# Feed-forward stage: the place of VectorE's mixes for the next batch among its maskings and additions

## The reference

```python
x_mixed = k[0] * xp[:, :-2] + k[1] * xp[:, 1:-1] + k[2] * xp[:, 2:]   # a mix over three positions
h = jnp.einsum('bsd,pdm->bspm', x_mixed, W1) + b1                     # 9 paths of 64
stacked_paths = jnp.einsum('bspm,pmd->bspd', h, W2) + b2
scores = jnp.tanh(x_mixed @ Wo1 + bo1) @ Wo2 + bo2
weights = jax.nn.one_hot(jnp.argmax(scores, axis=-1), P)              # one path per position
collapsed = jnp.einsum('bspd,bsp->bsd', stacked_paths, weights)
return _layernorm(x + collapsed, gamma, beta)
```

## Time and profile before

| what | value |
|---|---|
| median of the runs | 1507.09 us (three runs, 1502.43 to 1507.27) |
| the profiled execution, its own time | 1502.06 us |
| its span, first to last instruction | 1500.3 us |
| TensorE, weight loads, VectorE, ScalarE, GpSimd busy | 95%, 44%, 73%, 64%, 29% |
| mean granted clock of TensorE | 0.992 of full |

### The profile page before, as it was taken

One profiled execution on the slowest core, in us unless ns is written; L12 is line 12 of the kernel. 1 busy time (PEld: TensorE's weight loads), 2 busy tenths in 40 slices (PEclk: granted clock), 3 DMA queues, 4 the chain that ended last, 5 costly groups with the idle time before them and its releaser, 6 DMA issues. The chain is left out here.

```text
span 1500.3 us, 25145 instructions
## 1 busy us (share of the span) xinstructions
PE 1423.4 (95%) x8234; PEld 656.3 (44%) x8282; DVE 1102.5 (73%) x2647; ACT 960.6 (64%) x2121; POOL 431.4 (29%) x561
## 2 busy tenths in 40 slices
PE   7999989999999999999999999999988999999995
PEld 4665543333333333333333333333324666566654
DVE  3225658888888888888888888888733888878775
ACT  4655447777777777777777777777775445455532
POOL 3443232122133133133133133123243262122312
PEclk9999999999999999999999999999999999999998
DMA  7899674223643843842842842842714521110001
GB/s 224 265 296 292 205 217 111 87 63 95 156 89 95 181 92 90 185 93 85 190 93 80 195 94 74 200 95 66 143 23 130 92 85 57 43 56 28 15 29 43
DMA packets 166752, 178.20 MB, mean 119 GB/s; under 512 B 26397, under 2 KB 135784, under 8 KB 166632
## 3 DMA queue, kind: packets, MB, share of 16 engines
q1 hardware_dynamic: 158184, 168.31, 44.2%
q10 hardware_dynamic: 8448, 8.39, 1.7%
HBM read 109.79 MB, written 66.06 MB: 117 GB/s over the span
## 5 line engine op out<-in xcount | busy, mean ns | idle before, releaser
L975 ACT ACTIVATE a_probs<-a_ps_s 128x512 f32<-128x512 f32 (+3 forms) x1536 | 648.0, 499 | 232.2 <-PE a_ps_s L1077 228.5
L176 DVE CUSTOM_DVE_ANT_0 h_space<-a_ps_m,a_causal 128x640 f32<-128x640 f32 (+5 forms) x624 | 530.3, 888 | 94.5 <-PE a_ps_m L150 91.1
L1077 PE MATMUL a_ps_s<-s_qs,s_ks 99*128 99x512 bf16 (+3 forms) x1536 | 405.6, 329 | 6.5 <-ACT a_probs L975 4.7
L150 PE MATMUL a_ps_m<-s_ks,s_qs 96*128 96x512 bf16 (+3 forms) x1440 | 347.1, 326 | 9.1 <-DVE a_mx L176 2.3
L925 POOL TENSOR_SCALAR_AFFINE_SELECT a_probs<-a_probs 128x512 f32<-128x512 f32 x256 | 163.0, 637 | 664.6 <-ACT a_probs L975 664.6
L1035 PE MATMUL a_ps_o<-a_probs,s_vq 128*32 128x512 f32 (+3 forms) x3072 | 327.6, 497 | 10.1 <-POOL a_probs L925 4.2
L1077 PEld LDWEIGHTS a_ps_s<-s_qs,s_ks 99*128 99x128 bf16 x1536 | 137.0, 97 | 330.7 <-ACT a_probs L975 241.6
L150 PEld LDWEIGHTS a_ps_m<-s_ks,s_qs 96*128 96x128 bf16 x1440 | 122.6, 98 | 157.8 <-issue 57.9
L1547 PE MATMUL f_ps_o<-f_w,f_hm 128*128 128x256 f32 (+1 forms) x640 | 151.5, 385 | 0.9 <-DVE f_y L1454 0.9
L1547 PEld LDWEIGHTS f_ps_o<-f_w,f_hm 128*128 128x128 f32 (+1 forms) x640 | 121.5, 192 | 27.6 <-issue 8.4
L545 PE MATMUL p_ps_qk<-p_x_t,p_wqk 128*128 128x512 f32 x256 | 120.5, 600 | 0.1
(11 more groups left out here) (137 smaller groups left out, 1310.6 us busy)
## 6 DMA issues: line engine op xcount, KB each, us to landing
qk_parts<-h_space SPq DMA_DIRECT2D x64, 384.0 KB, 4.0
s_qs<-qk_parts SPq DMA_DIRECT2D x192, 128.0 KB, 2.8
s_ks<-qk_parts SPq DMA_DIRECT2D x192, 128.0 KB, 2.8
v_rows<-h_space SPq DMA_DIRECT2D x16, 896.0 KB, 6.1
s_vq<-v_rows SPq DMA_DIRECT2D x32, 448.0 KB, 4.5
f_x_in<-in_L_attn_x_dram ACTq DMA_DIRECT2D x16, 512.0 KB, 6.7
heads_out<-a_o_sb SPq DMA_DIRECT2D x128, 64.0 KB
f_x_in<-in_L_attn_x_dram SPq DMA_DIRECT2D x8, 1024.0 KB, 8.8
```

The source lines that it names most:

```text
L150: last = pe.matmul(out, self.qs[0:TROWS, j, h, q], self.ks[0:TROWS, j, h, s:s + wide], start=k == 0, stop=mask is None)
L176: taken = dve.tensor_tensor_reduce(out=shown[:, i % 2, k * CHUNK:k * CHUNK + width], in0=row, in1=self.causal[:, SEQ - width:SEQ], scale=1 ...
L975: act.activation(probs[:, st % PB, h, 0:width], ps_s[:, n % BANKS, 0:width], ACT.Exp, scale=SCALE).then_inc(exps[h % 2], 1)
L1077: pe.matmul(ps_s[:, n % BANKS, 0:width], ks[0:MROWS, j, h, kt * P:(kt + 1) * P], qs[0:MROWS, j, h, q0:q0 + width], start=True, stop=True)\
```

## The change

VectorE's two mixes of the next batch no longer stand ahead of the first addition of x. The first addition comes first, then maskings 0, 1 and 2, the first mix, maskings 3 and 4, the second mix, and the second addition of x. Nothing else of the program is different.

```diff
                         if c == 0 and not last:
                             layernorm(1 - e, 8 * (b + e) + 16, at)
-                        if c == 1 and not last:
-                            for k in range(KC):
-                                mix(b + 1, 1 - e, k, at)
                         if c or not first:
                             add_x1(n - 1, *((e, 0) if c else (1 - e, 1)), 0)
                         for i in range(MC):
                             keep_hidden(n, c, i)
+                            if c == 1 and not last and i in (2, LAST):
+                                mix(b + 1, 1 - e, i // LAST, at)
                         if c or not first:
                             add_x1(n - 1, *((e, 0) if c else (1 - e, 1)), 1)
```

## The result

The changed kernel takes 1531.3 us (median of six runs, 1528.54 to 1536.17) against 1506.94 us for the kernel before: a ratio of 1.0172 (95% interval 1.0151 to 1.0192), so it is slower by 1.7%. The profiled execution took 1530.69 us for a span of 1529.0 us, 28.7 more than the profiled execution before, with a mean granted clock of 0.983 instead of 0.992. (The two medians lie 24.4 us apart; the part on the prediction says why.)

What follows compares the result with a forecast made beforehand. TensorE, busy 95% of the span, was taken to bound the kernel. The profiled 1502.1 us plus 15.0 for later starts and 10.1 for clock falls gave 1527.2 us, range 1513 to 1535.

Steps and rivals of the forecast that it cites:

- turn 1: Batch 1's turn, where GpSimd sums the last batch's attention: later start +0.8 us, plus 1.4 for slowed mixing instructions.
- the clock: TensorE's granted clock falls behind the new stall in all seven turns, six more than before, 1.69 us each: +10.1 us.
- my first reading: If the other runs before had two or three more clock falls, the new kernel gains nothing on top; otherwise 1532 us.
- The bound: TensorE is busy 95% of the span, so what counts is where it stands still or newly could.
- The comparison of 5.02 us of mixing with 1.63 us of room: VectorE's two waits in a first chunk, 0.54 and 1.09 us, are the room for 5.02 us of moved mixes.
- A: Start of VectorE's first addition of x when only TensorE holds it back, 2.47 us after output tile 1 starts.
- The chain from A: VectorE's addition, maskings and both mixes: next hidden product at A + 8.98 against TensorE's own A + 5.21, 3.8 us stall.
- The collision that goes: First mixing instruction, 3.14 us beside GpSimd's addition of beta, takes 1.28 us in the new place in turns 2 to 6.
- everything else, at nothing: ScalarE's products, bank release, second addition, normalization, roots, store and first chunks: no cost beyond shifting along.
- The clock holds: Rival: TensorE's clock does not fall and only the later start counts, 1517.1 us; few falls or none 0.23.
- GpSimd's collision comes along: Rival: a GpSimd operation meets the mixes in every turn from 1 on, 11.2 us more, 1538.4; 0.10 with longer low stretches.
- not slower: Rival: the mixes fit into VectorE's waits among the maskings, at most the 10.5 us of stalls go, 1491.6 us; 0.07.

Runs made afterwards that it cites:

- both mixes in the middle: The changed kernel with both mixes placed between maskings 2 and 3: 1515.14 us, ratio 1.0084 to the kernel before.
- The filled stall: The changed kernel with four more f32 products on TensorE at the end of each second chunk: 1523.2 us, ratio 1.0121 to the kernel before.
- one mix in the room: Against the kernel before, first mix left ahead of the first addition of x, second mix put between maskings 2 and 3: 1491.38 us, ratio 0.9909.
- second mix late: Against the kernel before, first mix left ahead of the first addition of x, second mix put behind the last masking: 1503.38 us, ratio 0.9993.
- short and long sums: The changed kernel with GpSimd's last-batch summing operations on one of sixteen heads each (short, 1527.98 us), or with each of its additions done twice (long, 1534.47 us).
- addition first: Against the kernel before, only the first addition of x moved ahead of both mixes, the maskings after them: 1539.08 us, ratio 1.022.

## Why the prediction held, and where it was off

The predicted 1527.2 lies 4.1 us under the measured 1531.3, in the range, on the right side. Part of the closeness is luck. Against the 28.7 us between the profiled executions I had 25.1: turn 1 came out 4.1 us too low and 1.5 us outside the changed part were missing, while the clock was 1.4 and the other six turns together 0.5 us too high.

*The 5 us between the profiled execution before and its median: the clock.* I had left open whether they come from further falls. Of the twenty executions of the kernel before that were timed beside the experiments, the five with a mean granted clock of 0.992 or 0.993 took 1499.9 to 1502.6 us, and the nine at 0.988 or 0.989 took 1505.0 to 1506.6. A clock lower by 0.004 over 1505 us is worth 6 us, by an estimate as rough as the three digits of the clock, and the groups differ by 4.5 us. The profiled execution before, at 0.992, belongs to the faster group, while the changed kernel's (1530.69) is near its median. That fits my first reading, that the new kernel gains nothing on top: the medians lie 24.4 us apart instead of 28.7, and of these 24.4 the clock's part is smaller than 8.7.

*The bound: right. The comparison of 5.02 us of mixing with 1.63 us of room: right in its answer, wrong as a measure.* The order with one mix behind A loses its stalls; the orders with two behind A all gain one. But one mix is 2.5 us, more than 1.63, and it fits. Maskings 3 and 4 and the second addition of x may slip behind the start of the opening product, whose first half waits for none of them, so VectorE's idle time is less than the room. What decides is the chain from A up to the last thing that the product waits for: with one mix behind masking 2 it is A + 5.27, against TensorE's own A + 5.21.

*The chain from A: right.* Forecast and measured start of the opening product: A + 8.98 and 8.86 in the changed kernel, 7.78 and 7.68 with both mixes in the middle. With the second mix behind the last masking it was 6.47 and 6.97, where masking 3's wait was left out; with one mix in the room the 5.20 measured is TensorE's own and says only that the chain is no longer. The stall came out at 3.4 to 3.5 us instead of 3.8. In turn 3 the product starts 0.12 us earlier than the chain said, and the stall begins with the modelled end of the output tile at A + 5.36, 0.15 us behind the A + 5.21 at which the product would start beside it. Later starts in turns 0 and 2 to 6: 12.3 us, forecast 3.7 + 9.1 = 12.8.

*Turn 1: mis-sized.* I gave its later start 0.8 + 1.4 = 2.2 us, at most 3.6, with each mixing instruction losing 0.35 us as in the earlier trace rows. It was 6.3, and the wait that I had put at up to 5 us was 9.1. The step that failed is to carry the loss per instruction from a place where the mixes were under way before GpSimd's run to one where they arrive within it. The Trainium skill (SBUF — State Buffer, SBUF: two separate sides) lets the one that started first keep the ports for its whole instruction; I took from it one operation per mixing instruction as the most. Here the hold lasted for nine operations, and for seventeen with the run made longer.

*The clock: right in kind, 1.4 us too high.* Six more falls at 1.69 us, 10.1 in all, against 8.7: five falls and not seven, but two of them cost 2.6 to 2.7 us. The rule that idle gaps between bursts of matmuls send the clock down (the Trainium skill, TensorE: Matmul & The Clock Gate, Why this matters for your kernels) would have had all seven turns fall; the trace has two stalls of 3.4 to 3.5 us without a fall. The filled stall settles that the stalls are the cause.

*The collision that goes and "everything else, at nothing": right.* The first mixing instruction is back at 1.27 us outside turn 1; no wait in the first chunks appeared, and the distance from the last opening product to the end grew by 0.2 us.

*Rivals.* "The clock holds" is out by the windows; "GpSimd's collision comes along" happened in one turn of six, through another of its operations than the one I had named; "not slower" is out for this order, and its price, 1491.6 (the old stalls gone and nothing in their place), is close to the 1491.4 of the order with one mix in the room. *Not foreseen*: 1.3 us ahead of the changed part, which no edit touches. Over the nine profiles the fourth spreading of the very first chunk starts anywhere from 1144.2 to 1148.3 us, so a difference of that size between two single profiles says nothing of the change.

## What to carry to other kernels

When work is moved behind a wait to shorten one stall, add up the engine's chain from that wait to the last thing that the next consumer needs, and compare it with the time at which the consumer would start by itself. Here that is 5.27 us with one mix against 5.21, and 7.78 or 8.98 with two, so one mix of two fits. Keep the part that is ready ahead of the wait, and count the engine's idle time at the wait as given away: here 4.7 us a turn. And price a long stall of TensorE (here 3.4 us and up) with the slower matmuls that follow it: 8.7 of the 28.7 us between the two profiles were that.

## What the runs showed of the hardware

*Stalls of TensorE and its granted clock.* From the profiles of the nine kernels, in the second chunks of this stage, falls from 1.00 (2.4 GHz) to 0.50 (1.2 GHz) by the longest stall in one piece:

| stall, us | kernels | falls |
|---|---|---|
| 0.3 or less | one mix in the room; stall filled, without turn 1 | 0 of 13 |
| 1.3 to 2.5, ahead of the fourth spreading | before | 1 of 6 |
| 1.5 to 2.0 | second mix late | 0 of 7 |
| 2.2 to 2.3 | both in the middle | 0 of 6 |
| 3.4 to 3.5 | changed, short and long sums | 15 of 19 |
| 4.2 | addition first | 6 of 6 |
| 5.6 to 14.4 | turn 1 of changed, addition first, both in the middle, long sums, stall filled | 5 of 5 |

Behind a stall of 3.4 to 3.5 us a fall makes the next 3.7 us of matmuls 1.7 or 2.6 us longer; behind the longer ones of turn 1, 1.4 to 2.7. What separates the four of nineteen, and the one at 1.56 us, these runs don't tell.

*VectorE held by GpSimd.* A mixing instruction has two inputs in SBUF. In five kernels one arrived in turn 1 within an undisturbed run of GpSimd operations and stood until the run was over: 6.87 us in the changed kernel and with both mixes in the middle, 6.86 with the stall filled, 8.61 with the addition first, 12.23 with the longer run. In the other three with a full run there (the kernel before and the two orders with the first mix ahead of the addition) the first mix was under way as the run began. There the two engines took turns: GpSimd's operations took about 1.7 us instead of 0.7 beside a mixing instruction (once 2.1), and the mixing instructions 1.63 to 1.75 us. In those two orders the second mix took turns as well (1.40 and 1.63, and 1.27 and 1.63 us), though it came later, within GpSimd operations that had been back at 0.7 us. So what goes with taking turns here is a mixing instruction under way at the start of the run; why that should still count for a later one stays open.
